# Decoder kernel: first experts' rows in two PSUM banks, router sums by doubling, weight pieces 4 and 5 split one slot later

## What is computed

```
x = x + attn(layernorm(x))      # 8 layers, linear attention with feature maps, 16 heads of 64, hidden 1024, gelu
x = x + cross(layernorm(x), ctx)  # softmax attention over a context of 128 tokens, 16 heads of 16
x = x + ffn(layernorm(x))       # a shared SwiGLU (512 wide) plus one of 8 routed SwiGLU experts per token
```

## Time and profile before

| | us |
|---|---|
| median of 3 runs | 2924.09 (2919.79 to 2924.2) |
| the profiled execution | 2919.42 |
| its span | 2917.4 |
| PE busy in it | 2811.2 (96%) |
| DVE busy | 2417.1 (83%) |
| ACT busy | 1920.5 (66%) |
| POOL busy | 704.6 (24%) |

### The profile page before, as it was taken

One profiled execution on the slowest core, in us unless ns is written; L12 is line 12 of the kernel. 1 busy time (PEld: TensorE's weight loads), 2 busy tenths in 40 slices (PEclk: granted clock), 3 DMA queues, 4 the chain that ended last, 5 costly groups with the idle time before them and its releaser, 6 DMA issues. The chain is left out here.

```text
span 2917.4 us, 35444 instructions
## 1 busy us (share of the span) xinstructions
PE 2811.2 (96%) x12986; PEld 2324.3 (80%) x12986; DVE 2417.1 (83%) x3615; ACT 1920.5 (66%) x2839; POOL 704.6 (24%) x482
## 2 busy tenths in 40 slices
PE   5899999999999999999999999999999999999988
PEld 4688888888888888888888888888888877776777
DVE  7978898889888988888888888888989875776466
ACT  5667777776677777767776777677777763444255
POOL 2203231223122312321233123312322112100313
PEclk9899999999999999999999999999999999998999
DMA  3000101000100010101000100110010011101422
GB/s 123 20 1 28 31 5 37 22 23 19 37 22 23 19 37 12 33 19 37 12 31 21 37 6 22 35 37 6 23 32 23 2 32 41 51 1 50 179 40 36
DMA packets 62093, 92.00 MB, mean 32 GB/s; under 512 B 16480, under 2 KB 42336, under 8 KB 59744
## 3 DMA queue, kind: packets, MB, share of 16 engines
q1 hardware_dynamic: 57840, 85.46, 9.2%
q0 software_dynamic: 4080, 4.27, 0.9%
HBM read 80.24 MB, written 10.38 MB: 31 GB/s over the span
## 5 line engine op out<-in xcount | busy, mean ns | idle before, releaser
L804 PE MATMUL PS<-XTHI,WHI 128*128 128x512 f32 x1536 | 625.5, 407 | 19.5 <-DVE EX L1162 14.7
L806 PE MATMUL PS<-XTHI,WLO 128*128 128x512 f32 x1536 | 607.1, 395 | 0.0
L805 PE MATMUL PS<-XTLO,WHI 128*128 128x512 f32 x1536 | 602.7, 392 | 0.0
L1036 ACT ACTIVATE ATT<-INV,CC,CE 128x128 f32<-128x128 f32 x1024 | 432.7, 485 | 121.8 <-PE Y L846 115.5
L846 PE MATMUL Y<-WO,ATT 128*128 128x256 f32 x2048 | 455.7, 381 | 6.0 <-ACT ATT L1036 6.0
L846 PE MATMUL Y<-W2S,H 128*128 128x256 f32 x2048 | 458.1, 380 | 2.0 <-DVE T L1234 1.4
L846 PEld LDWEIGHTS Y<-WO,ATT 128*128 128x128 f32 x2048 | 391.6, 191 | 61.8 <-ACT ATT L1036 5.6
L846 PEld LDWEIGHTS Y<-W2S,H 128*128 128x128 f32 x2048 | 387.0, 190 | 55.5 <-DVE T L1234 1.8
L804 PEld LDWEIGHTS PS<-XTHI,WHI 128*128 128x128 f32 x1536 | 291.4, 190 | 84.3 <-issue 16.8
L1001 ACT ACTIVATE EX<-PS,BNEG 128x512 f32<-128x512 f32 x256 | 165.5, 684 | 292.5 <-DVE INV L1214 152.0
L806 PEld LDWEIGHTS PS<-XTHI,WLO 128*128 128x128 f32 x1536 | 290.7, 189 | 64.9
(11 more groups left out here) (211 smaller groups left out, 4786.4 us busy)
## 6 DMA issues: line engine op xcount, KB each, us to landing
STAGE<-L_attn_Wkvq SPq DMA_DIRECT2D x64, 384.0 KB, 3.1
WO<-L_attn_Wo SPq DMA_DIRECT2D x8, 1024.0 KB, 4.8
W2S<-L_attn_W SPq DMA_DIRECT2D x8, 1024.0 KB, 4.8
STAGE<-L_attn_W SPq DMA_DIRECT2D x32, 256.0 KB, 5.3
WGU<-L_ffn_r_gate SPq DMA_DIRECT2D x8, 512.0 KB, 9.8
WGU<-L_ffn_r_up SPq DMA_DIRECT2D x8, 512.0 KB, 9.5
WD<-L_ffn_r_down SPq DMA_DIRECT2D x8, 512.0 KB, 9.6
rows_in<-R SPq DMA_DIRECT2D x1, 3036.0 KB, 13.2
```

The lines of the kernel that those rows point to most:

```text
L804: nc.tensor.matmul(out, whi[:, kc, :], xhi[:, kc, :], start=(kc == 0), stop=False)
L805: nc.tensor.matmul(out, whi[:, kc, :], xlo[:, kc, :], start=False, stop=False)
L806: ins = nc.tensor.matmul(out, wlo[:, kc, :], xhi[:, kc, :], start=False, stop=(kc == KD - 1))
L1036: ins = nc.scalar.activation(ATT[:, 2 * p + i, ss], INV[:, b, i, ss], ACT.Identity, scale=CE[:, b, k:k + 1], bias=CC[:, b, k:k + 1])
```

## The change

It has three parts, which touch different stages.

1. **Pieces 4 and 5** are split in slot 3 with pieces 6 and 7, on both ACT and POOL, and no longer at the end of slot 2. Since there are three staging buffers, piece 7 can be loaded only when piece 4 has been released, which is now in the middle of that step.
2. **Router sums.** The 16 additions of 8 elements become four additions of 128 elements, which go back and forth between two buffers (distances 1, 2, 4 and 8), after two memsets of 64 elements. The copy of the totals from PSUM goes straight to the first buffer.
3. **First experts' rows.** Tile u = 1 is transposed into bank 7, without the wait for tile 0. ACT makes both high parts of the rows first, before it waits for the weights, and then the four weight parts; DVE makes both low parts of the rows, then all four low parts of the weights, and `added(3)` last.

```diff
-                    for k in range(6, HC):
+                    for k in range(4, HC):
                         low_part(l + 1, k)
...
-                if load and t == TILES - 2:
-                    for k in range(4, 6):
-                        low_part(l + 1, k)
...
-                    high_parts(l + 1, range(6, HC))
+                    high_parts(l + 1, range(4, HC))
...
-                    if load and t == TILES - 2:
-                        high_parts(l + 1, range(4, 6))
...
+    def turned(self, u):
+        return self.PSX[:, 7 if u == 1 else 6, 0:D]
...
     def turn(self, nc, pe, ident, u):
         pe.wait_ge(self.xu_in[u % 2], 16 * (u // 2) + 16)
-        if u > 0:
+        if u > 1:
             pe.wait_ge(self.xt_lo, u)
...
+            for u in range(2):
+                first.input_hi(nc, act, u)
             act.wait_ge(first.routed_in, 16 * 3 * E)
             act.wait_ge(u_mm, TILES * FC)
             act.wait_ge(eid, 1)
-            for m in range(2):
-                first.high(nc, 0, m)
             for u in range(2):
-                first.input_hi(nc, act, u)
-            for m in range(2):
-                first.high(nc, 1, m)
+                for m in range(2):
+                    first.high(nc, u, m)
...
-            then(nc.vector.tensor_copy(TOTS[:, :, :], PSX[:, 7, P:2 * P].rearrange("p (b e) -> p b e", e=E)))
-            then(nc.vector.memset(BASE[:, 0, :], 0.0))
-            for b in range(SEQS):
-                then(nc.vector.tensor_tensor(BASE[:, b + 1, :], BASE[:, b, :], TOTS[:, b, :], ALU.add))
+            nc.vector.memset(SUMA[:, 0:8, :], 0.0)
+            then(nc.vector.memset(SUMB[:, 0:8, :], 0.0))
+            then(nc.vector.tensor_copy(SUMA[:, 8:, :], PSX[:, 7, P:2 * P].rearrange("p (b e) -> p b e", e=E)))
+            for src, dst, d in ((SUMA, SUMB, 1), (SUMB, SUMA, 2), (SUMA, SUMB, 4), (SUMB, SUMA, 8)):
+                then(nc.vector.tensor_tensor(dst[:, 8:, :], src[:, 8:, :], src[:, 8 - d:8 - d + SEQS, :], ALU.add))
...
             dve.wait_ge(eid, 1)
-            for m in range(2):
-                first.low(nc, dve, 0, m)
             for u in range(2):
                 first.input_lo(nc, dve, u)
+            for u in range(2):
+                for m in range(2):
+                    first.low(nc, dve, u, m)
             added(TILES - 1)
-            for m in range(2):
-                first.low(nc, dve, 1, m)
```

More of the change, by code:

```diff
@@ L1438, in turn @@
         pe.wait_ge(self.xu_in[u % 2], 16 * (u // 2) + 16)
-        if u > 0:
+        if u > 1:
             pe.wait_ge(self.xt_lo, u)
         for kc in range(KD):
-            ins = nc.tensor.transpose(self.PSX[:, 6, kc * P:(kc + 1) * P], self.XU[:, u % 2, kc * P:(kc + 1) * P],
+            ins = nc.tensor.transpose(self.turned(u)[:, kc * P:(kc + 1) * P], self.XU[:, u % 2, kc * P:(kc + 1) * P],
                                       ident[:, :])
@@ L1452, in input_hi @@
         act.wait_ge(self.xt_mm, u + 1)
-        nc.scalar.copy(self.XTHI[:, u % 2, :, :], self.PSX[:, 6, 0:D].rearrange("p (c t) -> p c t", c=KD)
+        nc.scalar.copy(self.XTHI[:, u % 2, :, :], self.turned(u).rearrange("p (c t) -> p c t", c=KD)
                        ).then_inc(self.xt_hi, 1)
@@ L1464, in input_lo @@
         dve.wait_ge(self.xt_hi, u + 1)
-        nc.vector.tensor_tensor(self.XTLO[:, u % 2, :, :], self.PSX[:, 6, 0:D].rearrange("p (c t) -> p c t", c=KD),
+        nc.vector.tensor_tensor(self.XTLO[:, u % 2, :, :], self.turned(u).rearrange("p (c t) -> p c t", c=KD),
                                 self.XTHI[:, u % 2, :, :].bitcast(F32), ALU.subtract).then_inc(self.xt_lo, 1)
@@ L1500, in route @@
         IOT128 = behind_rows(2 * TOK + 6 * P, P, SEQS)
-        BASE = behind_rows(2 * TOK, (SEQS + 1) * E, E)
+        SUMA = behind_rows(2 * TOK, (8 + SEQS) * E, E)
+        SUMB = cross.ATT[:, 0, 0:(8 + SEQS) * E].rearrange("p (x a) -> p x a", a=E)
+        BASE = SUMA[:, 7:8 + SEQS, :]
         MORE = behind_rows(2 * TOK + 4 * P, P, SEQS)
```

## The result

| | before | after |
|---|---|---|
| median, measured together | 2922.56 us (4 runs) | **2898.7 us** (4 runs, 2892.01 to 2899.04) |
| the profiled execution | 2919.42 | 2898.52 |
| its span | 2917.4 | 2896.5 |

The ratio is 0.9909, 95% interval 0.9889 to 0.9929. Two later comparisons of the same two kernels gave 2899.19 and 2899.85 us, just inside it.

A forecast was written before the change was run, and what follows sets the result against it. PE, busy 96% of the span, was taken as the bound. Gains of 4.35, 2.35 and 10.9 sum to 17.6 us off the profiled 2919.4, giving 2901.8; plus 4.7 offset, 2906.5 us, range 2899 to 2916.

The forecast's parts named there:

- Part 1, tail of slot 2: End of slot 2: without two ACT copies and two POOL subtractions it matches slot 1's, 0.87 us per layer change, 6.1 gained.
- Part 1, charge for POOL: Slot 3: POOL's subtraction for piece 7 likely precedes DVE's L1198, delaying PE 0.25 us per layer change, 1.75 in all.
- 1.73 less 0.3: Slot 3: DVE's idle time of 1.73 us at L1156, some 0.3 of it only slot 2's own lateness.
- 1.75 us or none: Slot 3: whoever starts first holds the shared port for a whole instruction, so the charge is all or nothing.
- Part 2: Router sums in `route`: four additions end sooner, PE's first wait goes, `down(0)` starts earlier; 2.35 us gained, bounds 3.9 and 1.0.
- lower gain of 1.6: Router sums: by the lock rule each addition pays a full multiplication plus its own time, 4 x 0.87; gain 1.6 us.
- Part 3: End of `route`: earlier, shorter `down(3)` and shorter pause, 9.2 us; full clock afterwards, 1.7; together 10.9, lower bound 6.5.
- The offset: Whole kernel: the median of the runs lies 4.7 us above the profiled execution, kept in the forecast time.
- The low end of the range: Whole kernel: all upper bounds, 20.9 us off the profiled 2919.4, give 2898.5; the range begins at 2899.
- Only the tail gains: Rival: slot 3 gives back all 0.87 us per layer; time 2911 us, chance 0.12.
- the tail's clock: Rival, end of `route`: PE's clock falls or ACT's weight copies start late; Part 3 gives 6.5, time 2911; chance 0.09.
- The slower one: Rival, slot 3: piece 7's load lands late, each us beyond 1.5 counting one for one; time 2932 us, chance 0.04.

The follow-up runs named there:

- the short load: The changed kernel with piece 7's load cut to a quarter of its columns (outputs wrong, only times of use): 2908.58 us, one run.
- the version with pieces 2 to 5: The changed kernel with the splits of pieces 2 and 3 also moved, within slot 2, behind pieces 0 and 1: 2897.32 us, later 2886.68 us.

## Why the prediction was right and wrong

- **Part 1, tail of slot 2.** Forecast 7 x 0.87 = 6.1; measured 5.9 over seven slots, 5.8 net. Right, and so is the load of piece 7 being hidden (3.1 us to landing).
- **Part 1, charge for POOL: the step that failed in the sum, 1.75 us.** "Here POOL is likely first" was taken for all seven layer changes. It is an even draw: POOL was first in two of the seven in the profiled execution and in 44 of 91 over all profiles. The price was right where it applied: L1193 near 2.9 us, the slot up to 0.25 longer. By the short load DVE can take 1.3 us without loss, as the forecast's 1.73 less 0.3 says. So seven charges of 0.25 stand for two of about 0.15 and 0.1. The forecast read the lock's rule as one outcome for all, "1.75 us or none"; it falls anew in each layer.
- **Part 2.** 2.35 forecast, 2.8 measured. The additions advance in POOL's step, 0.62 to 0.70 us each, as forecast, and not by the 0.87 each that the forecast drew from the lock's rule for its lower gain of 1.6; the eight small sums cost 1.1 more beside POOL, not 1.6.
- **Part 3.** 9.2 + 1.7 forecast, 9.0 + 1.6 measured: `down(3)` starts 5.5 us earlier and takes 7.17, as forecast; the pause shrank by 1.7 us to 2.33, not by 2.0. The 1.6 is in part luck: with the same pause four of 15 profiles did not have it.
- **The sum.** These terms measure 5.8 + 2.8 + 9.0 + 1.6 = 19.2 for 17.6. **What the forecast put at nothing without a reason** are the stages that the change leaves alone, above all the one behind the stack, 5.5 us shorter by the two means over all profiles (2.3 in the first pair). I took a stage that the change doesn't touch as fixed.
- **The offset: wrong, 1.5 us.** "The median of the runs lies 4.7 above that execution, which I keep" made three runs into a property of the kernel. Beside the change before's median was 2922.56, 3.1 above it, and over the six comparisons it lies from 2921.2 to 2925.9. The miss of 7.8 us is thus 1.5 of offset, 1.6 of terms and 4.7 for which there was no term (23.9 between the medians less 19.2). The 23.9 is known to 5.8 us either way, and the two larger comparisons leave only 2.8 and 3.3 of the 4.7, so a part of it is luck. The low end of the range was made of upper bounds of terms alone, with nothing for the stages left alone; it came as near as it did because it was taken off the profiled 2919.4, without the offset that the forecast itself carried.
- **Rivals.** "Only the tail gains" and "the tail's clock" did not happen in the whole. The slower one is real as a mechanism: 3.4 us late, the load costs 1.8 us per layer.

## What to carry to other kernels

Charge a collision only with what exceeds the idle time of the engine behind it (here nothing for 1.3 us of delay, up to 0.25 us for 1.5 to 1.7), and only as often as it happens: where two engines arrive within 0.2 us of each other, look at every repetition in the trace and not at one. A pause removed from the bounding engine is worth its length, and whatever else stood beside it: look for the next pause of the same kind (pieces 2 and 3 gave 13 us by the same move). Before timing a difference of some us by parts, profile the unchanged kernel twice and see which stages repeat to 0.1 us and which vary by 7; for the latter give the range a term in both directions.

## What the runs showed of the hardware

- **Extra work that costs nothing, or less.** With 24 and 48 more products in the second tile that tile ended at 210.4 and 209.0 us, where it ends at 210.7 to 212.9 without them, and the 10.2 us stretch at 1.2 GHz that the changed kernel's first profile has there was gone. PE had been idle 5.45 us ahead of its transpositions in the changed kernel's trace and 0.97 in the one with 48 more; that the shorter pause kept the clock up fits, and is not shown by itself.
- **A disturbance in the middle of `route`, in seven profiles of 20.** In all seven of two sets that were measured together, none of the others, DVE's products for tile 1 of the shared part came late. In the version with pieces 2 to 5, disturbed, then undisturbed:

```profile
2710.64 0.69 DVE L1722 TENSOR_TENSOR W2S<-EX,PSX 128x512 f32<-128x512 f32 x1 [2.26 <-PE PSX L1617]
2719.18 0.69 DVE L1722 TENSOR_TENSOR W2S<-EX,PSX 128x512 f32<-128x512 f32 x1 [7.85 <-remote]
...
2719.92 10.10 PE L1634 MATMUL PSX<-R,W2S 128*128 128x256 f32 x32 [5.32 <-DVE W2S L1722]
```
```profile
2709.68 0.69 DVE L1722 TENSOR_TENSOR W2S<-EX,PSX 128x512 f32<-128x512 f32 x1 [0.90 <-PE PSX L1617]
2712.40 0.69 DVE L1722 TENSOR_TENSOR W2S<-EX,PSX 128x512 f32<-128x512 f32 x1 [2.03 <-PE PSX L1617]
```

  The two steps are 8.5 us apart for 2.7, "remote" names nothing in the trace, and PE's own records show 5.3 us of idle. The same seven profiles lack the landing times of the scattered rows, and five of them those of the routed weights' loads. It cost 3.2 to 8.5 us of the stage, whatever the kernel. Its cause is open; the two sets ran on two chips, one of which had shown nothing of it before, so it is not a property of one chip.
